# A two-layer metaformer block: token mixer channel by token, local norm in the channel layout, experts' pairwise sums on TensorE

## The reference

```python
x = x + conv0(ln_c(x), ...)      # state-space mixer over the 256 pixels of an image
t = t + ffn0(ln_t(t), ...)       # 8 experts, hidden 128, top 2 by softmax
x = x + conv1(ln_c(x), ...)      # divisive norm
t = t + ffn1(ln_t(t), ...)       # 8 experts, hidden 256, top 2

# conv0: xbcdt = u @ W_in -> x_ssm (128), B (16), C (16), dt (8 heads)
dA = softplus(dt + dt_bias) * -exp(A_log)
KV = einsum('bls,blhp->bhsp', B_ssm, V * dA[..., None])
y  = einsum('bls,bhsp->blhp', C_ssm, KV) + V * D_param[None, None, :, None]
y  = (y - mean(y)) / sqrt(var(y) + 1e-05) * ln_gamma + ln_beta     # over 128 channels
out = y @ W_out

# conv1: x2 = x * x; Pk mixes 8 channels of a group, Ps is a depthwise 3x3 sum without its centre
norm_pool = 1 / sqrt(Pk + Ps + (beta + 1e-6))
out = x * norm_pool * gamma_outside + beta_outside

# ffn: out += w_e * (gelu(x @ W1[e] + b1[e]) @ W2[e] + b2[e])   (exact gelu)
```

## Time and profile before

| | |
|---|---|
| median of 3 runs | 723.84 us |
| the profiled execution | 722.71 us, its span 720.9 us |
| mean granted TensorE clock | 0.924 |
| busy: PE, DVE, ACT, POOL | 522.0, 523.4, 378.9, 283.1 us |
| one period of 24 slots in the middle | 75.0 us |

### The profile page before, as it was taken

The page is one execution under the profiler, slowest core; times in us unless marked ns, Lnnn a source line. Parts: engine busy times, 40 slices in busy tenths (PEclk is TensorE's granted clock), DMA queues, the critical chain, the costliest instruction groups (busy, mean ns, idle before and its releaser), DMA issues.

```text
span 720.9 us, 10179 instructions
## 1 busy us (share of the span) xinstructions
PE 522.0 (72%) x3778; PEld 247.9 (34%) x3778; DVE 523.4 (73%) x926; ACT 378.9 (53%) x440; POOL 283.1 (39%) x240
## 2 busy tenths in 40 slices
PE   2314674578787988798777978797879876975766
PEld 1213232233333433344334333343334332431322
DVE  3266267859798879987988898889979796556413
ACT  2113712467476555756575657664766564643532
POOL 2122146125434463635452653365254433333013
PEclk9999965699998999999999999999999998998788
DMA  4600600063205140505032502450044005500130
GB/s 67 102 3 1 133 0 1 2 132 74 47 1 134 31 89 15 123 13 117 15 83 53 120 16 55 79 119 16 21 99 100 19 17 117 116 18 1 43 76 30
DMA packets 27841, 41.50 MB, mean 58 GB/s; under 512 B 11792, under 2 KB 19088, under 8 KB 27792
## 3 DMA queue, kind: packets, MB, share of 16 engines
q1 hardware_dynamic: 27152, 38.75, 26.2%
q0 software_dynamic: 640, 2.10, 1.0%
HBM read 38.22 MB, written 2.62 MB: 57 GB/s over the span
## 4 chain that ended last, share of the span: by engine, by line
DVE 37%; DMA 23%; PE 13%; issue 10%; POOL 8%; SPq 5%; ACT 4%; POOLq 0%; DVEq 0%; ACTq 0%
DMA WB<-w_scratch 19%; DVE nacc L1134 6%; PE yP L861 4%; PE hP L845 4%; SPq L402 3%; DMA w_scratch<-wTs 3%; DVE YW L1181 2%; POOL stat_c L486 2%; PE sA L760 2%; DVE xsplit L971 2%; PE sA L770 2%; DVE xcen_b L964 2%; POOL stat_b L486 2%; DVE xnrm L964 1%; POOL stat_d L486 1%
## 5 line engine op out<-in xcount | busy, mean ns | idle before, releaser
L691 ACT ACTIVATE H<-hP,b 128x1024 f32<-128x1024 f32 x192 | 209.3, 1111 | 82.4 <-PE hP L845 80.8
L861 PE MATMUL yP<-H,w 128*64 128x512 f32 x768 | 205.6, 618 | 28.5 <-DVE ACC L1181 25.1
L845 PE MATMUL hP<-xT,w 128*64 128x512 f16 x1536 | 212.4, 401 | 4.1 <-ACT H L691 4.0
L556 POOL TENSOR_TENSOR ACC<-ACC,YW 128x512 f32<-128x512 f32 x96 | 125.5, 1313 | 192.1 <-DVE YW L1181 192.1
L845 PEld LDWEIGHTS hP<-xT,w 128*64 128x64 f16 x1536 | 83.6, 114 | 128.0 <-issue 70.8
L1181 DVE SCALAR_TENSOR_TENSOR YW<-yP,b,WB 128x512 f32<-128x512 f32 x96 | 71.3, 744 | 31.9 <-PE yP L861 31.9
L861 PEld LDWEIGHTS yP<-H,w 128*64 128x64 f32 x768 | 54.0, 141 | 71.8 <-issue 38.1
L1134 DVE SCALAR_TENSOR_TENSOR nacc<-PAD,taps,nacc 128x256 f32<-128x256 f32 x112 | 60.5, 540 | 3.7
L1181 DVE SCALAR_TENSOR_TENSOR ACC<-yP,b,WB 128x512 f32<-128x512 f32 x32 | 23.1, 746 | 50.5 <-DMA WB<-w_scratch 50.5
L540 POOL TENSOR_SCALAR nrg<-nacc,go_col 128x512 f32<-128x512 f32 x8 | 12.6, 1573 | 69.1 <-ACT nacc L659 69.1
L578 ACT ACT_TABLE_LOAD x23 | 29.5, 1283 | 9.7 <-DVE nacc L1134 7.9
(11 more groups left out here) (144 smaller groups left out, 775.6 us busy)
## 6 DMA issues: line engine op xcount, KB each, us to landing
WB<-w_scratch SPq DMA_DIRECT2D x32, 1024.0 KB, 10.0
X<-in_x SPq DMA_DIRECT2D x8, 256.0 KB, 12.0
out<-X POOLq DMA_DIRECT2D x8, 256.0 KB, 2.8
H<-in_L_ffn_W SPq DMA_DIRECT2D x2, 512.0 KB, 6.6
H<-in_L_ffn_W SPq DMA_DIRECT2D x2, 256.0 KB, 4.2
w<-in_L_ffn_W SPq DMA_DIRECT2D x1, 512.0 KB, 4.9
w_scratch<-wTs SPq DMA_DIRECT2D x16, 32.0 KB, 1.8
w<-in_L_ffn_W SPq DMA_DIRECT2D x1, 256.0 KB, 4.1
```

Of the source, the lines that this page charges most:

```text
L556: pool.tensor_tensor(ACC[l][:, cols], ACC[l][:, cols], YW[:, u % 4, :], ALU.add).then_inc(summed, 1)
L691: nc.scalar.activation(H[:, s % RING, :], hP[s % 2][:, :], ACT.Gelu, bias=b1[l][:, e * ch + c:e * ch + c + 1], scale=1.0 / WS)\
L845: mm = nc.tensor.matmul(hP[s % 2][b * C:(b + 1) * C, hf * HALF:(hf + 1) * HALF], w1[l][:, sp, w, b * C:(b + 1) * C], xT[l][g % 2][:, hf * ...
L861: mm = nc.tensor.matmul(yP[hf][a * C:(a + 1) * C, :], w2[l][:, (2 * j + a) * ch + c, :], H[:, (2 * ch * j + 2 * c + a) % RING, hf * HALF:( ...
```

## The change

It has four parts.

1. **The mixer is computed channel by token.** y is produced with the 128 channels on partitions. The mean over the channels is taken out beforehand: of `KVs` by a new step of DVE (state: a reduce and a subtract), and of the V*D term by folding D and the mean into weights `wd`, so that V*D becomes an fp16 product of `xTa` inside y0 and y1. ACT writes the square `ysq` and the copy `yT`. PE sums the squares over channels by 8 matmuls with one column of ones (y_sums), DVE and POOL form the reciprocal root per token, mix_out multiplies float32 `yT` by float32 `wout_g` (8 matmuls in place of 32 in fp16), and DVE scales the result per token and adds `X0b` in a second instruction. The norm n, POOL's `Yd` and `ysplit`, the two turns and their copies are gone.
2. **The divisive norm stays in the channel layout.** ACT also writes `xg` (input times gamma) from the turned tiles, POOL multiplies it by the norm (`zT`), and after turn_u DVE only adds the residual. The 8 taps run over both halves at once (528 elements, the first tap in two pieces of 256 from PSUM).
3. **The experts' pairwise sum on PE.** `final` no longer turns `ACC` and lets DVE add the two halves of the partitions; it multiplies `ACC` by `fold` (two identities on top of each other), and one DVE add is left per half.
4. **The tables.** ab starts 36 slots ahead of its experts in place of 42 and ends in slot 0 in place of 1. Its front and its middle therefore stand 6 slots later against cd and the experts; sums_a and norm_a of DVE now stand in slots 19 and 22 (before 12 and 16), decay, values and state in 9 to 11 (before 3 to 5), y0 and y1 in 12 and 14 (before 6 and 8).

```diff
-    ab=dict(turn_a=12, proj0=17, proj1=19, proj2=20, c_cols=21, state=23, y0=24, y1=26, turn_hi=32,
-            turn_lo=34, mix_out=35, turn_b=38, gate=41, send=43),
+    ab=dict(turn_a=13, proj0=17, proj1=19, proj2=20, c_cols=21, state=23, y0=24, y1=26, y_sums=28,
+            mix_out=29, turn_b=32, gate=35, send=36),
...
-AB_LEAD = 42
+AB_LEAD = 36
...
+            pool.tensor_tensor(fold[:, :], ident32[:, 0:C], ident32[:, C:2 * C], ALU.add).then_inc(ident_made, 1)
...
+                elif k == "y_sums":
+                    pool.wait_ge(yvar.sem, yvar.at(g))
+                    pool.tensor_tensor(stat["n"][:, 3, :], stat["n"][:, 2, :], neg_half[:, :], ALU.pow)\
+                        .then_inc(yrs.sem, 1)
...
-                    pool.tensor_scalar(nrg[:, :, :, :], nrs[:, :, :, :], go_col[:, 0:1], None, ALU.mult)\
+                    pool.tensor_tensor(zT[:, :, :].rearrange("p q (r c) -> p q r c", r=SIDE), norms,
+                                       xg[:, :, :].rearrange("p q (r c) -> p q r c", r=SIDE), ALU.mult)\
                         .then_inc(nsc.sem, 1)
...
+                elif k in ("y0", "y1"):
+                    hf = int(k[-1])
+                    cols = slice(hf * HALF, (hf + 1) * HALF)
+                    act.wait_ge(ymm.sem, ymm.at(g, hf + 1))
+                    nc.scalar.activation(ysq[:, cols], sA[:, :], ACT.Square, scale=1.0 / WS).then_inc(yev.sem, 1)
+                    nc.scalar.activation(yT[:, cols], sA[:, :], ACT.Copy, scale=1.0 / WS).then_inc(yev.sem, 1)
...
+                    for q in range(2):
+                        nc.scalar.activation(
+                            xg[:, q].rearrange("p (n k) -> p k n", k=2),
+                            sC[:, q * 256:(q + 1) * 256].rearrange("p (k n) -> p k n", k=2),
+                            ACT.Copy, scale=go_col[:, 0:1]).then_inc(sqT.sem, 1)
...
-                    for t in range(4):
-                        mm = nc.tensor.matmul(sA[:, t * INNER:(t + 1) * INNER], ctS[q, t * P:(t + 1) * P],
-                                              KVs[q, (t // 2) * INNER:(t // 2 + 1) * INNER], start=True, stop=True)
+                    for t in range(2):
+                        for s in range(2):
+                            nc.tensor.matmul(sA[:, t * PIX:(t + 1) * PIX], wd[:, s, :],
+                                             xTa[:, hf * HALF + t * PIX:hf * HALF + (t + 1) * PIX],
+                                             start=(s == 0), stop=False)
+                        mm = nc.tensor.matmul(sA[:, t * PIX:(t + 1) * PIX], KVs[q, t * INNER:(t + 1) * INNER],
+                                              ctS[q, t * PIX:(t + 1) * PIX], start=False, stop=True)
...
+                    for t in range(T):
+                        mm = nc.tensor.matmul(sA[:, t:t + 1], ysq[:, t * P:(t + 1) * P], ones[:, 0:1],
+                                              start=True, stop=True)
...
-                        for n in range(4):
-                            mm = nc.tensor.matmul(sA[:, t * C:(t + 1) * C], yT[:, n // 2, t * P:(t + 1) * P],
-                                                  wout[:, n % 2, :], start=(n == 0), stop=(n == 3))
+                        mm = nc.tensor.matmul(sA[:, t * C:(t + 1) * C], yT[:, t * P:(t + 1) * P], wout_g[:, :],
+                                              start=True, stop=True)
...
-                    mm = nc.tensor.transpose(sC[:, t * P:(t + 1) * P], ACC[l][:, col:col + P], ident32[:, :])
+                    mm = nc.tensor.matmul(sC[:, t * C:(t + 1) * C], ACC[l][:, col:col + P], fold[:, :],
+                                          start=True, stop=True)
...
+                    v.tensor_reduce(kv_mean[:, :], state, AX, ALU.add).then_inc(kvC.sem, 1)
...
+                    v.tensor_tensor(X1[g % 2][:, :, :], sA[:, :].rearrange("p (t c) -> p t c", t=T),
+                                    per_tile(stat["n"][:, 3, :], C), ALU.mult).then_inc(x1s.sem, 1)
+                    dve.wait_ge(x1s.sem, x1s.at(g))
+                    v.tensor_tensor(X1[g % 2][:, :, :], X1[g % 2][:, :, :], X0b[:, :, :], ALU.add)\
                         .then_inc(x1v.sem, 1)
```

More of the change, by code:

```diff
@@ L61 @@
 ACT_AT = dict(
-    ab=dict(sums_a=7, turn_a=12, proj0=17, proj1=18, proj2=19, c_cols=21, decay=21, state=23, sums_n=28,
-            turn_hi=32, turn_lo=33, sums_b=36, turn_b=37, top2=41, send=42),
+    ab=dict(sums_a=5, turn_a=13, proj0=17, proj1=18, proj2=19, c_cols=21, decay=21, y0=24, y1=26,
+            sums_b=30, turn_b=31, top2=35, send=36),
     cd=dict(sums_c=1, turn_c=4, norms=9, sums_d=11, turn_d=14, top2=17, send=18),
@@ L66 @@
 DVE_AT = dict(
-    ab=dict(centre_a=0, sums_a=6, norm_a=10, decay=21, values=22, y0=25, y1=27, centre_n=28, sums_n=29,
-            norm_n=30, mix_out=35, centre_b=35, sums_b=36, norm_b=37, top2=41, weights=41),
+    ab=dict(centre_a=0, sums_a=7, norm_a=10, decay=21, values=22, state=23, y_sums=28, mix_out=29,
+            centre_b=29, sums_b=30, norm_b=31, top2=35, weights=35),
     cd=dict(centre_c=1, sums_c=1, norm_c=3, pool0=5, pool1=6, pool2=7, pool3=7, turn_u=10, centre_d=10,
@@ L72 @@
 POOL_AT = dict(
-    ab=dict(sums_a=7, norm_a=9, decay=25, state=26, sums_n=30, norm_n=31, sums_b=34),
+    ab=dict(sums_a=7, norm_a=9, state=26, y_sums=28, sums_b=29),
     cd=dict(sums_c=1, norm_c=2, scale=8, sums_d=12),
@@ L76 @@
 SP_AT = dict(
-    ab=dict(decay=22, send=41),
+    ab=dict(decay=22, send=35),
     cd=dict(send=21),
@@ L319, in sums_until @@
             return 6 * (u // 8) + max(0, u % 8 - 1)
-        A_USES = ("turn_a", "proj0", "proj1", "proj2", "c_cols", "state", "y0", "y1", "turn_hi", "turn_lo", "mix_out",
+        A_USES = ("turn_a", "proj0", "proj1", "proj2", "c_cols", "state", "y0", "y1", "y_sums", "mix_out",
                   "turn_b", "gate", "send")
@@ L341, in a_read @@
             count, k = {"turn_a": (trS["a"], 1), "proj0": (pjS, 1), "proj1": (pjS, 2), "proj2": (pjS, 3),
-                        "c_cols": (ctC, 1), "state": (kvS, 1), "y0": (yv, 1), "y1": (yv, 2), "turn_hi": (trS["n"], 1),
-                        "turn_lo": (trS["n"], 2), "mix_out": (x1v, 1), "turn_b": (trS["b"], 1), "gate": (gv[0], 1),
+                        "c_cols": (ctC, 1), "state": (kvC, 2), "y0": (yev, 2), "y1": (yev, 4), "y_sums": (yvar, 1),
+                        "mix_out": (x1s, 1), "turn_b": (trS["b"], 1), "gate": (gv[0], 1),
                         "send": (wts[0], 1)}[name]
@@ L614, in ab @@
                     act.wait_ge(ct.sem, ct.at(g))
[L615 removed]
+                    nc.scalar.activation(ctS[:, :], sA[0:64, :], ACT.Copy).then_inc(ctC.sem, 1)
                 elif k == "decay":
@@ L1137, in cd @@
+                    for n in range(max(1, 2 * part), 2 * part + 2):
+                        i, j = neighbours[n]
+                        dve.wait_ge(tap.sem, tap.at(g, n + 1))
+                        v.scalar_tensor_tensor(out=nacc[:, 0:rows, :], in0=PAD[:, i:i + rows, j:j + SIDE],
+                                               scalar=taps[:, 3 * i + j:3 * i + j + 1], in1=nacc[:, 0:rows, :],
+                                               op0=ALU.mult, op1=ALU.add).then_inc(tap.sem, 1)
                 elif k == "turn_u":
```

201 lines of the change are left out of this document (87 added, 114 removed).

## The result

The changed kernel takes 741.5 us (median of 4 runs, 739.66 to 745.84) where the kernel before takes 723.74 beside it (median of 4, 722.27 to 726.32). The ratio is 1.025, with a 95% interval of 1.0194 to 1.0306: it is slower, by 17.8 us. Forecast were 730 us, a range of 708 to 743, and a chance of 0.5 for slower.

What follows compares the result with a forecast made beforehand. The prediction took a period as a loop of waits, mostly paced by DVE's own list. 720.9 + 20.4 (six periods) - 11 (start) - 2.6 (end) = 727.7, plus 1.8 outside: 729.5, rounded to 730 us, range 708 to 743.

Steps and rivals of the forecast that it cites:

- the start: Up to the first send of layer 1: first weights out at 65 us, not 74.68; -11 us in all.
- step 1: Layer-1 weights' turn to final's second half: PE last, not WB; DVE's ACC pass starts at 16.3, +1.7 us.
- step 2: After y1, ACT's copies, DVE's sum and POOL's root put norm c's product at 22.8 to 23.1, +2.8 us.
- step 3: POOL's root of n, behind the root of c and X2b, delays mix_out to near 26.0; cumulative +4.0 us.
- step 4: xg puts two more ACT passes between turn_c and norm b's square, last there; cumulative +4.8 us.
- step 5: sums_a and norm_a now stand where DVE is the pace, +1.8; taps give back 0.9; cumulative +5.7 us.
- step 6: During top2, POOL's zT and norm_a's lo_part slow DVE, +1.2; layer 0's weights out at 52.9, +6.9 us.
- Step 7: Layer 0's send to the next: turn_u waits 2 us behind the weights' turn; 25.5 us for 29.0, -3.5.
- Rival C: PE falls to the low clock after waiting 7 to 8 us for gate weights: 748 us, chance 0.14.
- A: PE not late, float32 pairs costing 0.05 us: period 75.1 us, 709 us in all, chance 0.24.
- B: DVE's busy time is the bound, so a period loses 10 us: 650 us, chance 0.05.
- D: Start and periods cancel, periods +1.5 us each, 9 against 13.6: 718 to 722 us, chance 0.12.

Runs made afterwards that it cites:

- a_old_final: Changed kernel with the float32 fold undone, final turning both halves with transposes and DVE adding twice as before: 734.69 us, ratio 1.0148.
- a_ysq_fp16: Changed kernel with y's squares and the ones they are multiplied with in fp16 instead of float32: 727.9 us, ratio 1.0074.
- a_old_slots: Changed kernel with group a's norm put back in the slots of the kernel before, ab starting 42 slots ahead: 753.76 us, ratio 1.0415.
- a_best_b: Changed kernel with fp16 ysq, old final, early group 1 input, norm a in DVE's wait, POOL's root of a behind its ACC add: 702.24 us, ratio 0.9715.
- a_free_slots: Changed kernel with group a's sums_a and norm_a where DVE waits for final's second half, group 1's input early: 746.38 us, ratio 1.0311.
- a_best: Changed kernel with norm a in DVE's wait, POOL's root ahead of its ACC add, fp16 ysq, old final, early group 1 input: 732.66 us, ratio 1.0116.
- a_turn_u_first_b: Changed kernel with only PE's turn of layer 0's gate weights one slot later, behind turn_u, ACT's copy unmoved: 752.69 us, ratio 1.0404.
- b2_taps_only: Kernel before with only the taps over both halves, xg on ACT, zT on POOL, no xnrm product on DVE: 714.44 us, ratio 0.9884.

## Why the prediction came out as it did

The direction was right, and the time (741.5) lies in the range. The forecast of 730 was 11.5 us low. Against the forecast span of 727.7 the profile's 744.1 has 16.4 more: 10.2 in the six periods (+30.6 for +20.4), 3.3 in the start (-7.7 for -11), 3.3 in the last stretch (+0.75 for -2.6), less 0.4.

*Busy time.* DVE 54.8 for 55, PE 67.0 for 65 in a period. The float32 price of 0.12 us was right: final 1.10 for 1.1, mix_out 2.00 for 2.1, the sums 1.95 for 2.1. Of y0 and y1 only the size was off: 1.9 for 1.4 each; a float32 instruction with 16 rows and 256 columns takes 0.31, not the 0.12 of the others.

*The marks of the walk.* How much later each came than before, in us of the period:

| | forecast | measured |
|---|---|---|
| step 1, ACC pass | +1.7 | +1.9 |
| step 2, norm c's product | +2.8 to 3.1 | +3.3 |
| step 3, end of mix_out | +4.0 | +5.0 |
| step 4, norm b's sum | +4.8 | +5.9 |
| step 5, start of top2 | +5.7 | +7.05 |
| step 6, send of layer 0 | +6.9 | +7.95 |

The whole miss of this half, 1.05 us, is there at mix_out.

*Steps 1 and 2, right.* The ACC pass came 16.45 us into the period (forecast 16.3), behind PE and not behind WB. Norm c's product came at 23.35 (22.8 to 23.1). In the sum of step 1 y0 took 0.5 more and the wait for values 0.3 less (0.57 for 0.9). That PE is last there is shown by a_old_final.

*Step 3, the right place but the wrong waiter.* I had POOL's root of n last, mix_out from 26.0. It started at 27.0, for PE. What I left out is PE's own list: behind y1, which ended at 17.8 (forecast 17.6), stand two slots of experts, the sums, another slot and mix_out's product, without a gap:

```profile
420.83 0.69 PE L773 MATMUL sA<-ctS,KVs 16*128 16x256 f32 x2
421.45 1.05 PE L847 MATMUL hP<-xT,w 128*64 128x512 f16 x8
...
430.67 1.05 PE L847 MATMUL hP<-xT,w 128*64 128x512 f16 x8
```

The sums (425.02) and mix_out's product (428.74) are in the rows above. With my own prices that is 17.6 + 3.5 + 2.1 + 1.8 + 2.1 = 27.1. With the sums shortened (a_ysq_fp16) POOL is last, as forecast, and mix_out starts at 26.3. Step 4 behind it was right: +0.9 for +0.8.

*Steps 5 and 6, right in sum.* Step 5 added 1.2 (forecast 0.9), step 6 0.9 (forecast 1.2). In top2 three passes took 0.90, 1.19 and 0.93 in place of 0.22, beside POOL's low part, zT and an add into ACC: 2.4 us. But the kernel before had two such passes there, which I had left out:

```profile
438.90 0.68 DVE L1004 TENSOR_TENSOR gt<-gt,iota_m 128x64 f32<-128x64 f32 x1
...
440.39 1.33 DVE L1021 TENSOR_TENSOR gt<-gt 128x64 f32<-128x64 f32 x1
```

They cost 1.6, so that the meetings brought 0.8 and not 1.2. One of the six taps took 2.50 us in place of 0.77, while POOL issued a store and then ran its add. That the norm's place has a price is shown by a_old_slots (1.65 us to the send of layer 0), and a_best_b leaves 2.75 for it if its parts add up. That a place under DVE's wait is free whatever stands in the other lists was my mistake twice, in a_free_slots and a_best.

*Step 7, right in kind.* DVE waits 4.64 us at turn_u (forecast 2), WB is last (wait 0.83, forecast 2 to 3), from send to send 26.09 (forecast 25.5). The terms that I listed add up to 25.2, not 25.5, so that the whole sum should have read some 728 us. The reason for the long wait at turn_u is the half clock behind PE's wait: yP, hP and turn_u take 4.75 us there (457.31 to 462.06). Rival C had this mechanism and its place; the way of WB pays for it, as a_turn_u_first_b shows by moving it.

*The start, mis-sized.* The y products, the sums and mix_out took the times of half clock: 3.4 us for each half of y, where I had 2.8 for both, 3.54 for the sums where I had 3, and 3.68 for mix_out. The first group's mix_out ended at 47.0, not 45, the first weights left at 67.44, not 65. That is 2.4 of the 3.3 us. From there to the send at 136.06 it was 0.4 less than forecast, and from that to 163.43 1.2 more.

*The last stretch.* -2.6 was right for the work: a_ysq_fp16, whose code there is the same since no mixer runs any more, takes 57.82 us, -2.55. In both profiles PE waits 1.76 us ahead of norm c's turn and 1.61 ahead of the mix product. In the changed kernel half clock follows, in the other it doesn't. The mix product and the slot behind it, first in the changed kernel, then in a_ysq_fp16:

```profile
665.15 2.04 PE L811 MATMUL sC<-PAD,mix 128*128 128x512 f32 x2 [1.61 <-ACT xg L649]
667.12 1.92 PE L847 MATMUL hP<-xT,w 128*64 128x512 f16 x8
```

```profile
648.88 1.10 PE L814 MATMUL sC<-PAD,mix 128*128 128x512 f32 x2 [1.61 <-ACT xg L650]
649.91 1.05 PE L850 MATMUL hP<-xT,w 128*64 128x512 f16 x8
```

From the mix product to turn_u it takes 17.3 us in the one and 14.3 in the other, 3.0 of the 3.3 us (61.12 for 57.82). What decides it is open, and so is whether it made this execution the longest of the four, since only it was profiled.

*The rivals.* A (PE not late) fell with the price of final, the sums and y. B fell: DVE lost 11 us of busy time a period and the period grew by 5. The Trainium skill's rule to optimise the engine of highest occupancy first ("Perfetto Trace Analysis", Identifying the Most-Contended Engine) would have taken this change; the trace speaks against it here, though not against every part: b2_taps_only, which also takes work off DVE, gained 9 us. D (start and periods cancel) needed 1.5 us a period, and it was 5.1.

On TensorE the Trainium skill ("TensorE: Matmul & The Clock Gate", Weight-path perf modes) says that the fast weight load is for types other than FP32. The runs agree in kind: eight fp16 loads with one column each take 0.35 us where the sixteen float32 instructions take 1.95. The estimate of 1.7 us in the prediction, worked out from that page, was 0.25 to 0.3 low.
